# Mixture-of-experts attention block: a sine product on GpSimd waits for a sum on VectorE

## The chip, the core and the metric

The kernel runs on one core of one Trainium2 chip, as a single launch. The metric is the device time in microseconds (us). The core has engines that each run their own instruction queue in order and meet only through semaphores: TensorE (PE, matrix products), VectorE (DVE), ScalarE (ACT), GpSimd (POOL) and SyncE (SP, which starts transfers here). SBUF is the on-chip memory that they all read; PSUM is where TensorE leaves its products.

## The reference, cut to what matters

Input x is (4, 512, 256). It is normalised over its last axis, and the output is x plus an attention over 16 heads of size 128 plus a feed-forward part with eight routed experts (two chosen per row) and a shared one. The attention, with the rotation that the change touches:

```python
def _apply_rope(x, start_pos):
    ...
    x1 = x[..., 0::2]
    x2 = x[..., 1::2]
    r1 = x1 * cos - x2 * sin
    r2 = x1 * sin + x2 * cos
    return jnp.stack([r1, r2], axis=-1).reshape(B, T, H, Dh)
...
q = _apply_rope(q, 0)
k = _apply_rope(k, 0)
scores = jnp.einsum('bqhd,bkhd->bhqk', q, k) * scale
scores = jnp.where(causal[None, None, :, :], scores, jnp.float32(-jnp.inf))
attn = jax.nn.softmax(scores, axis=-1)
out = jnp.einsum('bhqk,bkhd->bqhd', attn, v).reshape(B, T, H * Dh)
return out @ wo
```

## The kernel before

All matrix products run in fp32, each as three products of a high and a low part (`hi*hi`, `hi*lo`, `lo*hi`). ScalarE writes the high part, and VectorE or GpSimd subtracts it to get the low one.

The attention is worked off as 64 heads m (a batch and a head each, `SLOTS`). The loop over steps s is software-pipelined and written out in each engine's own order: in step s, TensorE finishes head s, has the scores of heads s+1 and s+2 computed, and projects the key of head s+3 and the query of head s+4. One 128-row tile of the feed-forward part goes through most steps (s = -3 to 51). Routing (which experts each row takes) is computed by VectorE in steps 0 to 3; in steps 3 to 10 GpSimd sends the rows to a sorted table, four scatters a step; the rows come back by gathers on GpSimd, two a step from step 53, and sixteen in step 61.

The rotation of a query (which = 0) or a key (which = 1) of head m:

- TensorE projects into `qk_bank` (`project`).
- ScalarE copies it with its halves exchanged to `swapped[:, which]` (`swap`, L725).
- GpSimd multiplies `swapped[:, which]` by the sine table (`sin_product`, L876).
- VectorE multiplies `qk_bank` by the cosine table into `rot[:, which]` (`cos_product`, L1117).
- The two are added: for the query by VectorE (`rotate` in the vector block, L1124), for the key by GpSimd (`rotate` in the gpsimd block, L884).
- ScalarE writes the high part `qk_hi` (`rot_parts`, L734), GpSimd the low part `qk_lo` (`rot_parts`, L891).

`qk_bank` is one bank, so TensorE projects the key only after the query has been copied and multiplied, and the next query only after the key has.

GpSimd's queue in step s, in this order: sine product of the key of s+3, sum of the key of s+3, low part of the query of s+3, low part of its key, sine product of the query of s+4, and then weights, scatters or gathers of that step. VectorE's queue in step s holds, among much else: `row_max(s + 2, 3)` (L1133), the query's sum of s+3 (L1124), routing instructions in steps 0 to 3, the cosine product of the key of s+3 (L1117), two gating products, more maxima, the low parts of the transposed probabilities (L1148), two sums into the output rows (L1171), and last the cosine product of the query of s+4. ScalarE's queue in step s holds, around the rotation: `swap(s + 3, 1)`, an exponential, `rot_parts(s + 3, 0)`, copies, `rot_parts(s + 3, 1)`, `pt_parts(s + 1, 1)` (L756), `swap(s + 4, 0)`.

The routing instructions that the prediction names are L1030 (score, a scale and shift), L1035 (a maximum over the experts), L1036 and L1038 (comparison and product) in step 0, and L1072 (a copy) and L1074 (four sums) in step 2. L911 is a gather. L1228 adds gathered rows to the output.

Of the kernel before, what the change touches and what calls it, by code (L numbers as in the profile page):

```python
# [65 lines left out]
def moe_attention_kernel(nc, x_d, attn_d, ffn_d, wdown_d, gate_d, cos_d, sin_d, mask_d, ident_d,  # L66
                         iota_d, sel_d, out_d):
    with ExitStack() as ctx:
# [6 lines left out]
        def sem(name):  # L75
            return ctx.enter_context(nc.semaphore(name))
# [101 lines left out]
        cosm_ok, sinm_ok, rot_ok, rhi_ok, rlo_ok = ([sem(f"{n}_{x}") for x in "qk"] for n in (  # L178
            "cosm_ok", "sinm_ok", "rot_ok", "rhi_ok", "rlo_ok"))
# [37 lines left out]
        def exists(m):  # L217
            return 0 <= m < SLOTS
# [623 lines left out]
        def _(pool):  # L842
# [29 lines left out]
            def sin_product(m, which):  # L872
                if not exists(m):
                    return
                pool.wait_ge(swap_ok, 2 * m + which + 1)
                pool.tensor_tensor(swapped[:, which, :], swapped[:, which, :], sin_t[:, :],  # L876
                                   ALU.mult).then_inc(sinm_ok[which], 1)

# [36 lines left out]
            for s in range(-LEAD, SLOTS):  # L915
                q, r = prep(s)
                sin_product(s + 3, 1)
                rotate(s + 3, 1)
                rot_parts(s + 3, 0)
                rot_parts(s + 3, 1)  # L920
                sin_product(s + 4, 0)
                if s == -LEAD:
                    shared_parts()
                if r == 2:
                    weights_low(q)
                for n in scatter_steps(s):
                    scatter(n)
                for n in gather_steps(s):
                    gather(n)
                if s == -LEAD + 1:  # L930
                    pool.tensor_scalar(before[:, :], mask[:, T - P:T], -1.0, None, ALU.is_lt).then_inc(const_ok, 1)
# [434 lines left out]
```

## Time and profile before

| what | value |
|---|---|
| median of 3 runs | 805.72 us (805.53 to 807.64) |
| profiled execution, its own time | 804.73 us |
| its span | 802.9 us |
| mean granted clock of TensorE | 0.961 |
| busy: TensorE | 721.2 us (90%) |
| busy: VectorE | 664.4 us (83%) |
| busy: ScalarE | 593.2 us (74%) |
| busy: GpSimd | 504.2 us (63%) |
| sine products on GpSimd (L876) | 128, 175.7 us busy, mean 1372 ns |
| GpSimd idle just before them | 194.1 us |

The span is the time from the first to the last instruction of the profiled execution; its own time is 1.8 us more. A share of busy time is a mean over stages that differ: whether a delay counts is read from the chain of waits, which follows back from the last instruction what each had to wait for. A timeline row has the start in us from the span's start, the duration in us, the engine, the line, the operation with what it writes and reads, and in brackets how long the engine was idle before it and what ended that. An instruction may start some hundredths before the one ahead of it on its engine has ended.

### The profile page before, as it was taken

The numbers are of one execution on the slowest core, as the hardware profiler recorded it, in microseconds if no ns is written. First come the engines' busy times: TensorE is split into PE (matmuls) and PEld (weight loads), VectorE is DVE, ScalarE is ACT, GpSimd is POOL, SyncE is SP. The second block draws the span as 40 slices with busy tenths as digits, with TensorE's granted clock in tenths as the row PEclk, the third lists the DMA queues.
The fourth block names the chain that finished last, engine by engine and source line by source line (L and its number), as shares of the span: only waits on it lengthen the run. The fifth ranks groups of instructions, "written<-read, shape, count | busy, mean of one in ns | idle before, by whom it ended". The sixth has DMA issues, their size and how long they took to land.

```text
span 802.9 us, 15524 instructions
## 1 busy us (share of the span) xinstructions
PE 721.2 (90%) x4618; PEld 646.5 (81%) x4618; DVE 664.4 (83%) x1740; ACT 593.2 (74%) x1462; POOL 504.2 (63%) x413
## 2 busy tenths in 40 slices
PE   4798859898888999999999999999999999998633
PEld 3787758787777999999999999999999998886532
DVE  7667998888887888898888888988888888888526
ACT  3456647776876889888888888888888888886410
POOL 3444445888874666666656667666666667997730
PEclk9899998999999999999999999999999999999955
DMA  9342212344326445644445445644555430111212
GB/s 304 127 153 85 82 53 72 116 138 142 110 79 206 134 148 152 190 141 132 147 139 172 145 150 151 186 130 143 144 170 143 149 102 8 29 38 54 68 50 78
DMA packets 62066, 99.60 MB, mean 124 GB/s; under 512 B 9840, under 2 KB 34464, under 8 KB 61984
## 3 DMA queue, kind: packets, MB, share of 16 engines
q1 hardware_dynamic: 58912, 90.22, 36.8%
q0 software_dynamic: 3072, 8.39, 3.2%
q8 instruction: 38, 0.62, 0.3%
q14 instruction: 44, 0.36, 0.1%
HBM read 72.12 MB, written 26.48 MB: 123 GB/s over the span
## 4 chain that ended last, share of the span: by engine, by line
PE 66%; DVE 11%; POOL 10%; issue 5%; ACT 4%; another core or an unknown queue 2%; DMA 1%; DVEq 0%; SPq 0%; ACTq 0%; POOLq 0%
PE u_acc L403 13%; PE qk_proj L403 13%; PE scores L403 12%; PE ffn L403 10%; PE out_acc L403 8%; PE probs_t L509 7%; POOL swapped L876 3%; POOL qk_lo L891 2%; POOL rot L884 2%; DVE acc L1228 2%; DVE acc L1171 1%; POOL xs_sorted L900 1%; PE ffn L590 1%; PE ffn L564 1%
## 5 line engine op out<-in xcount | busy, mean ns | idle before, releaser
L876 POOL TENSOR_TENSOR swapped<-swapped,sin_t 128x512 f32<-128x512 f32 x128 | 175.7, 1372 | 194.1 <-ACT swapped L725 193.8
L891 POOL TENSOR_TENSOR qk_lo<-rot,qk_hi 128x512 fp32r<-128x512 f32 x128 | 165.4, 1299 | 26.6 <-ACT qk_hi L734 24.9
L1148 DVE TENSOR_TENSOR pt_lo<-probs_t,pt_hi 128x512 fp32r<-128x512 f32 (+3 forms) x256 | 125.4, 490 | 65.8 <-ACT pt_hi L756 64.1
L756 ACT ACTIVATE pt_hi<-probs_t 128x512 fp32r<-128x512 f32 (+3 forms) x256 | 111.8, 437 | 70.8 <-PE probs_t L509 39.0
L745 ACT ACTIVATE probs<-scores,nbias 128x512 f32<-128x512 f32 (+3 forms) x256 | 134.9, 527 | 36.6 <-DVE nbias L1133 35.1
L725 ACT ACTIVATE swapped<-qk_proj 64x512 f32<-64x512 f32 x256 | 151.9, 593 | 7.1 <-PE qk_proj L403 2.6
L1133 DVE CUSTOM_DVE_ANT_0 scores<-scores,mask 128x512 f32<-128x512 f32 (+3 forms) x256 | 125.3, 490 | 24.0 <-remote 13.2
L509 PE MATMUL probs_t<-ident,probs 128*128 128x128 f32 x640 | 114.5, 277 | 26.1 <-DVE pt_lo L1148 24.3
L1171 DVE SCALAR_TENSOR_TENSOR acc<-out_acc,rsum,acc 128x256 f32<-128x256 f32 x256 | 111.1, 476 | 8.4 <-remote 3.9
L509 PEld LDWEIGHTS probs_t<-ident,probs 128*128 128x128 f32 x640 | 81.0, 142 | 45.2 <-DVE pt_lo L1148 30.3
L884 POOL TENSOR_TENSOR rot<-rot,swapped 128x512 f32<-128x512 f32 x64 | 82.4, 1288 | 19.3 <-DVE rot L1117 11.0
L403 PE MATMUL scores<-qk_hi 128*128 128x512 f32 (+3 forms) x256 | 94.4, 369 | 0.0
L403 PE MATMUL u_acc<-pt_hi,c_hi 128*128 128x512 f32 (+3 forms) x256 | 89.4, 349 | 0.0
L1117 DVE TENSOR_TENSOR rot<-qk_proj,cos_t 128x512 f32<-128x512 f32 x128 | 87.3, 682 | 1.3 <-ACT swapped L725 1.2
L734 ACT ACTIVATE qk_hi<-rot 128x512 fp32r<-128x512 f32 x128 | 80.8, 631 | 4.8 <-POOL rot L884 4.2
L403 PE MATMUL u_acc<-pt_hi,c_lo 128*128 128x512 f32 (+3 forms) x256 | 84.2, 329 | 0.0
L403 PE MATMUL u_acc<-pt_lo,c_hi 128*128 128x512 f32 (+3 forms) x256 | 83.8, 328 | 0.0
L403 PE MATMUL scores<-qk_hi,qk_lo 128*128 128x512 f32 (+3 forms) x256 | 83.3, 325 | 0.0
L403 PE MATMUL scores<-qk_lo,qk_hi 128*128 128x512 f32 (+3 forms) x256 | 83.1, 325 | 0.0
L403 PE MATMUL out_acc<-m_hi,u_hi 128*128 128x256 f32 x256 | 79.0, 309 | 2.7 <-DVE u_lo L1156 2.4
L403 PE MATMUL out_acc<-m_hi,u_lo 128*128 128x256 f32 x256 | 73.5, 287 | 0.0
L403 PE MATMUL out_acc<-m_lo,u_hi 128*128 128x256 f32 x256 | 73.4, 287 | 0.0
(173 smaller groups left out, 1836.1 us busy)
## 6 DMA issues: line engine op xcount, KB each, us to landing
wt<-expert_parts SPq DMA_DIRECT2D x39, 704.0 KB, 4.5
wt<-expert_parts SPq DMA_DIRECT2D x39, 512.0 KB, 4.2
raw_a<-in_attn SPq DMA_DIRECT2D x8, 768.0 KB
xs_sorted<-u_lo SPq DMA_DIRECT2D x3, 1664.0 KB, 7.0
xs<-xs_sorted SPq DMA_DIRECT2D x39, 128.0 KB, 3.6
ys_sorted<-ysb SPq DMA_DIRECT2D x39, 128.0 KB, 4.0
expert_parts<-split SPq DMA_DIRECT2D x8, 352.0 KB, 2.3
expert_parts<-raw_f SPq DMA_DIRECT2D x8, 352.0 KB
```

Of the source, the lines that this page charges most:

```text
L403: last = pe.matmul(out, a, b, start=start and n == 0, stop=stop and n == 3 * len(pairs) - 1, **kw)
L509: last = pe.transpose(pt_bank[:, (i - j) * P:(i - j + 1) * P], probs[:, m % 2, a:a + P], ident[:, :])
L725: last = ac.activation(swapped[64 * half:64 * half + 64, which, :], qk_bank[64 - 64 * half:128 - 64 * half, :], ACT.Copy)
L745: ac.activation(probs[:, m % 2, PR_AT[i]:PR_AT[i] + n], s_bank[i % 2][:, 0:n], ACT.Exp, bias=nbias[:, m % 2, i:i + 1], scale=-1.0, accum_o ...
L756: ac.activation(pt_hi[:, PT_AT[j]:PT_AT[j] + n], pt_bank[:, 0:n], ACT.Copy).then_inc(pthi_ok, 1)
L876: pool.tensor_tensor(swapped[:, which, :], swapped[:, which, :], sin_t[:, :], ALU.mult).then_inc(sinm_ok[which], 1)
L884: pool.tensor_tensor(rot[:, which, :], rot[:, which, :], swapped[:, which, :], ALU.add).then_inc(rot_ok[which], 1)
L891: pool.tensor_tensor(qk_lo[:, m % 2, which, :], rot[:, which, :], f32(qk_hi[:, m % 2, which, :]), ALU.subtract).then_inc(rlo_ok[which], 1)
L1117: ve.tensor_tensor(rot[:, which, :], qk_bank[:, :], cos_t[:, :], ALU.mult).then_inc(cosm_ok[which], 1)
L1133: ve.tensor_tensor_reduce(a, a, mask[:, T - n:T], -SCALE, 3e38, ALU.add, ALU.min, nbias[:, m % 2, i:i + 1]).then_inc(max_ok, 1)
L1148: ve.tensor_tensor(pt_lo[:, c], pt_bank[:, 0:n], f32(pt_hi[:, c]), ALU.subtract).then_inc(ptlo_ok, 1)
L1171: ve.scalar_tensor_tensor(out=a, in0=out_bank[h][:, n, :], scalar=rsum[:, m % 4, i:i + 1], in1=a, op0=ALU.mult, op1=ALU.add).then_inc(add_ ...
```

## The change

The sine product of a key on GpSimd waits, besides for ScalarE's copy, until VectorE has added the two rotated parts of the query of the same head (`rot_ok[0]`, which L1124 raises). Both the sum and the product read SBUF only. No engine's sequence of instructions is altered; the second wait is an entry of its own in GpSimd's queue. The sine product of a query has no new wait. Behind the waiting instruction stand, on GpSimd, the key's sum, the two low parts and everything later.

```diff
--- before.py
+++ after.py
@@ -873,6 +873,9 @@
                 if not exists(m):
                     return
                 pool.wait_ge(swap_ok, 2 * m + which + 1)
+                if which == 1:
+
+                    pool.wait_ge(rot_ok[0], m + 1)
                 pool.tensor_tensor(swapped[:, which, :], swapped[:, which, :], sin_t[:, :],
                                    ALU.mult).then_inc(sinm_ok[which], 1)
```

## Rows read from the trace of the kernel before

**Rows 1.** The page: shares of the chain of waits by engine.
```profile
PE 66%; DVE 11%; POOL 10%; issue 5%; ACT 4%; another core or an unknown queue 2%; DMA 1%; DVEq 0%; SPq 0%; ACTq 0%; POOLq 0%
```

**Rows 2.** Timeline, head 31, steady stretch: start, us, engine, instruction.
```profile
410.71 0.69 DVE L1124 TENSOR_TENSOR rot<-rot,swapped 128x512 f32<-128x512 f32 x1
...
411.04 1.51 POOL L876 TENSOR_TENSOR swapped<-swapped,sin_t 128x512 f32<-128x512 f32 x1 [2.92 <-ACT swapped L725]
...
412.70 1.28 POOL L884 TENSOR_TENSOR rot<-rot,swapped 128x512 f32<-128x512 f32 x1
...
414.58 0.64 ACT L734 ACTIVATE qk_hi<-rot 128x512 fp32r<-128x512 f32 x1
```

**Rows 3.** Timeline, head 0.
```profile
29.50 0.68 DVE L1124 TENSOR_TENSOR rot<-rot,swapped 128x512 f32<-128x512 f32 x1
29.52 1.82 POOL L876 TENSOR_TENSOR swapped<-swapped,sin_t 128x512 f32<-128x512 f32 x1 [6.88 <-ACT swapped L725]
```

**Rows 4.** Chain of waits, heads 58 and 59: start, us, what.
```profile
694.07 1.33 POOL swapped L876
...
695.53 1.30 POOL rot L884
696.83 2.50 POOL qk_lo L891 x2
699.33 1.25 POOL swapped L876
...
700.73 0.99 POOL xn L911
...
704.44 1.30 POOL rot L884
```

**Rows 5.** Timeline, from head 58's ScalarE copy to head 59's product.
```profile
696.86 0.63 ACT L734 ACTIVATE qk_hi<-rot 128x512 fp32r<-128x512 f32 x1 [0.27 <-POOL rot L884]
...
699.16 0.68 DVE L1117 TENSOR_TENSOR rot<-qk_proj,cos_t 128x512 f32<-128x512 f32 x1
...
702.38 0.69 DVE L1124 TENSOR_TENSOR rot<-rot,swapped 128x512 f32<-128x512 f32 x1
...
703.00 1.30 POOL L876 TENSOR_TENSOR swapped<-swapped,sin_t 128x512 f32<-128x512 f32 x1
```

**Rows 6.** Timeline, heads 55 and 56.
```profile
668.85 1.30 POOL L884 TENSOR_TENSOR rot<-rot,swapped 128x512 f32<-128x512 f32 x1
...
670.18 0.63 ACT L734 ACTIVATE qk_hi<-rot 128x512 fp32r<-128x512 f32 x1 [0.22 <-POOL rot L884]
...
676.02 1.52 POOL L876 TENSOR_TENSOR swapped<-swapped,sin_t 128x512 f32<-128x512 f32 x1 [2.13 <-ACT swapped L725]
```

**Rows 7.** Chain of waits, heads 3 and 5.
```profile
74.67 1.24 DVE ysb L1030
...
76.58 0.30 DVE pick L1038
...
104.88 1.24 DVE xs L1072
```

**Rows 8.** Timeline, head 7.
```profile
136.61 0.69 DVE L1124 TENSOR_TENSOR rot<-rot,swapped 128x512 f32<-128x512 f32 x1
...
139.50 1.31 POOL L876 TENSOR_TENSOR swapped<-swapped,sin_t 128x512 f32<-128x512 f32 x1
```

**Rows 9.** Timeline from head 63 on; the last row is the chain's.
```profile
742.32 1.51 DVE L1124 TENSOR_TENSOR rot<-rot,swapped 128x512 f32<-128x512 f32 x1
743.75 0.68 DVE L1117 TENSOR_TENSOR rot<-qk_proj,cos_t 128x512 f32<-128x512 f32 x1
...
744.51 1.28 POOL L884 TENSOR_TENSOR rot<-rot,swapped 128x512 f32<-128x512 f32 x1 [1.23 <-DVE rot L1117]
...
769.78 0.95 POOL L911 DMA_INDIRECT wt<-ys_sorted,place  x1 [0.30 <-issue]
...
762.25 11.80 another core or an unknown queue
```

## The prediction

> **Names.** Head m is one of the 64 pairs of batch and head, in the order of `where`. Per head: D is VectorE's sum for the query (L1124), S GpSimd's sine product for the key (L876, the instruction that gets the new wait), C VectorE's cosine product for the key (L1117), G GpSimd's sum for the key (L884), A ScalarE's copy of the rotated key (L734), X GpSimd's two subtractions (L891).
>
> **What bounds the kernel now.** I read the chain of waits first, then timelines of VectorE, GpSimd and ScalarE around every S. TensorE holds 66% of the chain and GpSimd 10% [rows 1]. The reader is to see that GpSimd is not on it evenly. In heads 15 to 54 the chain is TensorE alone, with GpSimd idle before S. From head 56's S (676.02) to head 62's G it is GpSimd alone: S, G, two X, the next query's product, two gathers, and again [rows 4]. The change touches only S, so two questions decide: how much later does S end, and is that absorbed.
>
> **How much later S ends.** In the steady stretch S starts at 411.04, while D runs until 410.71 + 0.69 = 411.40 [rows 2]. With the wait it starts after D. The lag from VectorE's last event to a GpSimd start I take from head 63: C ends at 743.75 + 0.68 = 744.43 and G starts at 744.51, so 0.08 [rows 9]. The new start is 411.48, 0.44 later. But S is now stretched by the overlap: 1.51 us, against 1.30 where it meets only the last 0.07 of D [rows 2, 5]. At head 0 the two start 0.02 apart and S takes 1.82, ending 1.16 after D's end (30.18); in the steady stretch it ends 1.15 after [rows 2, 3]. So a product that overlaps is held until shortly before D ends. Afterwards it takes 1.30 at most, say 1.29, from 0.08 after D, ending 1.37 after: **0.22 us later**, not 0.44.
>
> By the Trainium skill's page "SBUF — State Buffer", section "Who interferes with whom", whichever of the two engines starts first keeps the shared ports for its whole instruction and the other is fully blocked. Taken literally, a held S would end 1.29 after D, and the wait would cost the lag of 0.08 alone; the sum below would be lower by 2 x 0.14 = 0.3. The rows show 1.15, and I go by them.
>
> **Heads 15 to 54, 40 heads: nothing.** S's delay moves G, which ends at 412.70 + 1.28 = 413.98, but A, which needs it, starts at 414.58 [rows 2]. ScalarE is late there by 0.60, more than 0.22. If the cover were gone, it would be 40 x 0.22 = 8.8 us: the slower end.
>
> **Heads 7 to 14: 0.1.** S starts at 139.50, long after D (136.61 + 0.69) [rows 8]; scatters stand ahead of it in GpSimd's queue. The wait is met, and leaves only one more entry in GpSimd's queue, between nothing and the lag of 0.08; I take 0.01 for each of 8 heads, near nothing since the engine has a scatter to work on meanwhile, and round up. Bounds 0 and 0.6.
>
> **Heads 0 to 6: -0.5.** Two things turn round here. Where S began first, D waited for it (as at head 63, 1.51 instead of 0.69 [rows 9]); heads 4 and 6 look so too, but TensorE has no gap there, so I count nothing. Where D began first, the routing instruction behind D waited for S: at head 3 the one of L1030 takes 1.24 on the chain, at head 5 the one of L1072 also 1.24, where a routing instruction of that size takes 0.30 (L1038) [rows 7]. With S behind D they come through first: 0.95 each, and VectorE holds the chain. But two and four more routing instructions with two inputs in SBUF follow. They now meet S themselves and end just after it, so most of it is given back: at head 3 S would end 1.37 after D, at 76.04, where the third instruction of the row now ends at 76.88; two of 0.30 that can only end behind 76.04, the first of them nearly done by then, end at 76.5 (D ends where L1030 begins on the chain, at 74.67). That is 0.4; at head 5, with S again at its end, 0.1. Together -0.5, bounds 0 and -1.9.
>
> The same page and section says that a VectorE instruction with two SBUF inputs contends with a GpSimd instruction that reads SBUF, and a reduction does not. That speaks for giving back; without it the term would be -1.9 and the sum -0.5.
>
> **Heads 55 and 56: +0.4.** Here G's delay is no longer covered: G of head 55 ends at 668.85 + 1.30 = 670.15 and A starts at 670.18 [rows 6]. A's delay goes to ScalarE's next copies, VectorE's C for the next query and TensorE's projection. Head 56's S (676.02, 1.52 long) is the chain itself [rows 6]. Two times 0.22, less a little slack: 0.4, bounds 0.2 and 0.44.
>
> **Heads 57 to 62: +0.9.** GpSimd comes to S only when its gathers are out, at 703.00, and D ends at 702.38 + 0.69 = 703.07 [rows 5]. Looked at alone the wait costs 0.15 once. But D itself follows from the G before: G ends at 696.83, A starts at 696.86, C at 699.16 and D at 702.38 [rows 4, 5], with every engine passing it on at once. So the delay comes round. The new loop is G to D's end, 703.07 - 695.53 = 7.54, plus 0.08, plus S 1.30, plus 0.14 from S to G (694.07 + 1.32 to 695.53) = 9.06. The old loop is 704.44 - 695.53 = 8.91 [rows 4, 5]. That is **0.15 a head, six times**. If a step of the way from G to D had slack, it would be 0.15 once: the lower bound.
>
> **Head 63 and the tail: 0.** D waited for S and took 1.51; now 0.69, so VectorE and ScalarE gain 0.82. GpSimd does not: D would end at 743.01, S at 743.09 + 1.29 = 744.38, G starts 0.14 later at 744.52, against 744.51 [rows 9]. The 18 gathers behind it, to the one at 769.78, keep their place. VectorE stands from 762.25 for 11.80 us for a queue that the profile does not name [rows 9], until 774.05, when the last gather must just have landed. So the end follows GpSimd, and the 0.82 is lost in that stall. What is lost before goes through whole.
>
> **Sum.** 0.1 - 0.5 + 0.4 + 0.9 = +0.9 us. The profiled execution is 804.73 us (span 802.9 and 1.8 around it), so 805.6; the median of the runs is 805.72, so I forecast **806.6 us**.
>
> **Rivals.**
> First, the other side of my forecast: VectorE's release pays in full. The routing instructions behind do not meet S (-1.9 instead of -0.5), and the tail follows VectorE, so head 63 gives -0.8. Then 0.1 - 1.9 + 0.4 + 0.9 - 0.8 = -1.3: 804.4, faster. It decides if L1036 and L1074 run beside S at 0.3. For it speaks that VectorE holds the chain at heads 3 and 5 [rows 7]; against it the stretched pairs in [rows 2, 3].
> Second, slower: the 0.22 is not covered in the steady stretch, +8.8 and so some 815. It decides if A is ready before G. Against it stand 0.60 us in every such head.
> Third, and faster too, the stall in the tail is not bound to the gathers' end. VectorE reaches it 0.8 us earlier than GpSimd does its gathers, and might get a piece of work done before it. From 774.05 to the span's end at 802.9 there are 29 us of work; 4 of them done within the stall would give 802.6.
> Fourth, the change does next to nothing: the loop has slack, each part is met, 805.8. Against it the shared start of S and D in 40 heads [rows 2].
>
> **Numbers.** My forecast 0.62 (its own range 805.6 to 807.6), the first rival 0.18, the second 0.07, the third 0.06, the fourth 0.07. The range 804.2 to 808.2 takes in my forecast, the first rival and the fourth, and leaves out the other two, 0.13, and some of the edges. About 0.3%, 2.4 us, is what a measurement of this kernel can tell from no change. Within it lie the forecast, the first and the fourth, less their edges: 0.83. Slower by more: the second and an edge, 0.10. Faster by more: the third and an edge, 0.07.
>
> **What would show it.** S starts 0.08 after D in heads 15 to 62 and takes 1.29 to 1.31; S and D never overlap, and D is never longer than 0.7. G to G in the steady heads is what it was, and some 9.06 in heads 57 to 62. At head 3 the L1030 instruction takes 0.3 and the one behind the next is long. G of head 62 lies some 0.9 later than it did. I am wrong if the loop of heads 57 to 62 stays at 8.91, if the steady heads grow, or if the stall of the tail starts or ends elsewhere against the gathers.

## The result, and the profile after

| | before | after |
|---|---|---|
| median | 805.87 us (20 runs, 805.16 to 808.89) | 809.61 us (20 runs, 804.48 to 814.73) |
| ratio | | 1.0040 (95%: 1.0024 to 1.0057) |
| profiled execution, its own time | 804.73 us | 814.73 us |

The kernel became slower by 0.4%, some 3.2 us, where 0.9 was forecast; that is above the 0.3% from which a loss can be told, which had a chance of 0.10. The change as a whole was timed twice more, on two chips: 1.0041 (1.0023 to 1.0059, run all1) and 1.0023 (1.0003 to 1.0043, all2). The three together give 1.0036, uncertain by 0.0010: **2.9 us, give or take 0.8**. That is the number to explain, not the 10 us between the two profiled executions: the one of after is the slowest of its 20 runs. Of its 10 us, 7.2 lie before G of head 17 (270.16 against 262.93), in a stretch that varies between executions of one and the same kernel (last section), 1.5 lie between heads 54 and 62, 0.1 in the step to head 63 and 1.2 behind it.

The page of after: the chain's shares, and the group of the sine products.

```profile
PE 66%; DVE 13%; POOL 7%; issue 6%; ACT 4%; another core or an unknown queue 2%; DMA 1%; DVEq 0%; SPq 0%; ACTq 0%; POOLq 0%
...
L879 POOL TENSOR_TENSOR swapped<-swapped,sin_t 128x512 f32<-128x512 f32 x128 | 165.4, 1292 | 222.4 <-DVE rot L1127 177.1
```

Against [rows 1] GpSimd has gone from 10% of the chain to 7%, and VectorE and the issue share have grown by as much: GpSimd is waited for less, because it now waits itself. The sine product's mean fell from 1372 to 1292 ns, so it is hardly ever stretched any more (3 of the 128 take over 1.32 us), and what GpSimd waits for before it is now VectorE's sum. (Lines behind the edit have moved by 3 in after and by 2 or 3 in the experiments.)

Timeline of after, head 31, in the steady stretch.

```profile
417.66 0.69 DVE L1127 TENSOR_TENSOR rot<-rot,swapped 128x512 f32<-128x512 f32 x1
...
418.49 1.29 POOL L879 TENSOR_TENSOR swapped<-swapped,sin_t 128x512 f32<-128x512 f32 x1 [3.43 <-DVE rot L1127]
...
419.92 1.30 POOL L887 TENSOR_TENSOR rot<-rot,swapped 128x512 f32<-128x512 f32 x1
...
421.52 0.64 ACT L734 ACTIVATE qk_hi<-rot 128x512 fp32r<-128x512 f32 x1
```

D ends at 418.35 and S starts at 418.49: 0.14 later, not the 0.08 of the forecast. S ends 1.43 after D's end, where the held S of [rows 2] ended 1.15 after it: **0.28 later, not 0.22**. G ends at 421.22, and A starts 0.30 after that, where it was 0.60. The cover holds, and is half used up. From G of head 17 to G of head 54 it takes 394.68 us before (262.93 to 657.61) and 394.68 after (270.16 to 664.84): nothing of the delay is passed on there.

Timeline of after, from D of head 59 to A.

```profile
710.28 0.69 DVE L1127 TENSOR_TENSOR rot<-rot,swapped 128x512 f32<-128x512 f32 x1
...
711.11 1.30 POOL L879 TENSOR_TENSOR swapped<-swapped,sin_t 128x512 f32<-128x512 f32 x1 [0.25 <-DVE rot L1127]
...
712.55 1.29 POOL L887 TENSOR_TENSOR rot<-rot,swapped 128x512 f32<-128x512 f32 x1
713.88 0.63 ACT L734 ACTIVATE qk_hi<-rot 128x512 fp32r<-128x512 f32 x1 [0.49 <-POOL rot L887]
```

The chain of waits of after, one turn of the loop, from G of head 58 to G of head 59.

```profile
703.42 1.31 POOL rot L887
...
704.75 0.05 ACT qk_hi L734
...
705.29 0.48 ACT pt_hi L756
...
705.80 0.57 DVE pt_lo L1151
...
707.14 0.74 PE u_acc L403 x3
...
707.88 0.93 PE qk_proj L403 x3
...
708.93 0.71 PE scores L403 x3
...
710.28 0.14 DVE nbias L1136
710.42 0.55 DVE rot L1127
710.98 0.02 issue
711.00 0.02 POOLq L878
711.02 0.10 issue
711.11 1.31 POOL swapped L879
...
712.44 0.02 POOLq L886
```

In [rows 4] this turn was GpSimd alone. Now the chain leaves GpSimd at G and comes back to it at S: through ScalarE (A, and the copy of the probabilities behind A), VectorE, TensorE, the maximum of scores, and D. This is the loop that the prediction priced, though its middle runs through ScalarE's probability copy (L756) and the scores, not through C. A turn is 712.55 - 703.42 = 9.13 (G in the timeline above and in the chain): G to D's end 7.55, then 0.14, S 1.30, and 0.14 to G. The forecast had 7.54, 0.08, 1.30 and 0.14. The one term that differs is the lag. The chain shows what it is made of: an entry of 0.02 in GpSimd's own queue (L878, the new wait) with 0.02 before it and about 0.10 behind. S to G has the same shape (L886) and the same 0.14, before and after: there the wait for S is an entry of its own too.

Timeline of after, head 63, and the last gather.

```profile
751.07 0.69 DVE L1127 TENSOR_TENSOR rot<-rot,swapped 128x512 f32<-128x512 f32 x1
751.68 0.68 DVE L1120 TENSOR_TENSOR rot<-qk_proj,cos_t 128x512 f32<-128x512 f32 x1
751.91 1.28 POOL L879 TENSOR_TENSOR swapped<-swapped,sin_t 128x512 f32<-128x512 f32 x1 [4.28 <-DVE rot L1127]
753.34 1.28 POOL L887 TENSOR_TENSOR rot<-rot,swapped 128x512 f32<-128x512 f32 x1
...
778.83 0.95 POOL L914 DMA_INDIRECT wt<-ys_sorted,place  x1 [0.30 <-issue]
```

The longest piece of the chain of waits of after in the tail.

```profile
772.65 10.39 another core or an unknown queue
```

D is 0.69 where it was 1.51 [rows 9], and G follows S, as forecast. The stall ends at 783.04, 3.3 us after the last gather is out (779.78); before, 774.05 against 770.73, 3.3 too. VectorE's 0.82 shows no gain at the end. The distance of 3.3 us is not the same in every run (last section).

### The profile page after: what moved, and what is told of

Read it like the earlier page. It is cut to its first block, busy times and chain, and to the rows that moved or that the text cites. A ratio compares the mean times of both kernels' runs of the same rounds, so it can differ in the third digit from the quotient of the medians.

```text
span 812.9 us, 15588 instructions
## 1 busy us (share of the span) xinstructions
PE 729.2 (90%) x4618; PEld 653.3 (80%) x4618; DVE 663.3 (82%) x1740; ACT 593.5 (73%) x1462; POOL 492.9 (61%) x413
## 4 chain that ended last, share of the span: by engine, by line
PE 66%; DVE 13%; POOL 7%; issue 6%; ACT 4%; another core or an unknown queue 2%; DMA 1%; DVEq 0%; SPq 0%; ACTq 0%; POOLq 0%
PE u_acc L403 13%; PE qk_proj L403 13%; PE scores L403 12%; PE ffn L403 10%; PE out_acc L403 8%; PE probs_t L509 7%; POOL swapped L879 3%; POOL rot L887 2%; POOL xs_sorted L903 2%; DVE acc L1174 2%; DVE acc L1231 2%; PE ffn L590 1%; DVE pt_lo L1151 1%; PE ffn L564 1%
## 5 line engine op out<-in xcount | busy, mean ns | idle before, releaser
L879 POOL TENSOR_TENSOR swapped<-swapped,sin_t 128x512 f32<-128x512 f32 x128 | 165.4, 1292 | 222.4 <-DVE rot L1127 177.1
L756 ACT ACTIVATE pt_hi<-probs_t 128x512 fp32r<-128x512 f32 (+3 forms) x256 | 111.8, 437 | 74.6 <-PE probs_t L509 43.8
```

Source lines behind the costliest of these rows:

```text
L756: ac.activation(pt_hi[:, PT_AT[j]:PT_AT[j] + n], pt_bank[:, 0:n], ACT.Copy).then_inc(pthi_ok, 1)
```

## The experiments

One table from the traces carries the argument. It gives, in us, the time from G of head 54 to G of head 62, the mean turn from head 56 to 62, the step from G of 62 to G of 63, and beside them the timed ratio. All three are differences of starts of G in the timeline.

| run | 54 to 62 | per head | 62 to 63 | ratio (95%) |
|---|---|---|---|---|
| before | 73.53 | 8.91 | 13.37 | |
| same_kernel | 73.53 | 8.91 | 12.47 | 0.9996 (0.9980 to 1.0012) |
| after | 75.07 | 9.12 | 13.43 | 1.0040 (1.0024 to 1.0057) |
| all1 | 75.00 | 9.11 | 13.41 | 1.0041 (1.0023 to 1.0059) |
| all2 | 75.06 | 9.12 | 13.43 | 1.0023 (1.0003 to 1.0043) |
| early | 73.46 | 8.90 | 13.22 | 0.9992 (0.9978 to 1.0006) |
| mid | 73.22 | 8.90 | 12.47 | 1.0004 (0.9985 to 1.0023) |
| late | 75.33 | 9.12 | 13.42 | 1.0039 (1.0022 to 1.0056) |
| late62 | 75.32 | 9.12 | 13.35 | 1.0040 (1.0025 to 1.0054) |
| late57 | 74.77 | 9.12 | 13.20 | 1.0021 (1.0004 to 1.0038) |
| late63 | 73.49 | 8.90 | 12.73 | 0.9993 (0.9977 to 1.0009) |
| waits_swapped | 74.67 | 9.06 | 13.38 | 1.0007 (0.9992 to 1.0022) |
| waits_swapped2 | 74.59 | 9.05 | 13.37 | 1.0009 (0.9987 to 1.0031) |
| padding | 74.40 | 9.06 | 13.33 | 1.0015 (1.0000 to 1.0029) |
| padding2 | 75.21 | 9.19 | 13.34 | 1.0017 (0.9997 to 1.0037) |
| sum_first | 74.40 | 9.13 | 12.27 | 1.0026 (1.0012 to 1.0040) |
| sum_early | 72.81 | 8.90 | 12.26 | 0.9997 (0.9982 to 1.0013) |
| early_sum_no_wait | 73.20 | 8.92 | 12.13 | 0.9994 (0.9980 to 1.0008) |
| late_gathers | 73.06 | 8.83 | 8.83 | 1.0103 (1.0078 to 1.0128) |
| late_gathers_wait | 74.99 | 9.11 | 9.11 | 1.0160 (1.0140 to 1.0180) |

### Where the loss is: the wait for some heads only

The whole change again, then the wait for a part of the heads:

```diff
+                if which == 1:                      # all1
+                if which == 1 and m <= 6:           # early
+                if which == 1 and 7 <= m <= 54:     # mid
+                if which == 1 and m >= 55:          # late
+                    pool.wait_ge(rot_ok[0], m + 1)
```

> The whole change once more. Loop theory: heads 57 to 62 run at 9.12 us each in every execution instead of 8.91, heads 55 and 56 lose 0.3 each, nothing else moves by itself, so the kernel is 1.5 to 2 us slower than before in executions with the same granted clock (some 807.5), and what is more than that comes with a lower mean clock. Clock theory: the wait itself brings more stretches at half clock in the stage up to 260 us; then the median is again some 4 us above before, and the trace again has half-clock stretches near 65 and 235 us.

> The wait for heads 0 to 6 alone. Loop theory: 805.5 to 806, no change (at head 3 the two-input instruction behind takes the place of the stretched one, 0.3 gained; heads 4 and 5 lose 0.2). Clock theory: most of the loss is here, because heads 0 to 6 shift TensorE's idle stretches: 808 to 809.

> The wait for heads 7 to 54 alone. Loop theory: no change, 805.9, as the key's sum is ready before ScalarE asks for it in heads 15 to 54 and the wait is met in heads 7 to 14. Clock theory: 806 to 808, if the half-clock stretch near 235 us comes from the entries in GpSimd's queue at heads 7 to 14.

> The wait for heads 55 to 63 alone. Loop theory: all of the steady loss is here, 807.4 to 807.9, with 9.12 us from sum to sum in heads 57 to 62. Clock theory: below 807.5, a third of the loss or less.

Measured on one chip: before 804.54, all1 807.87, early 804.30, mid 805.35, late 808.20. The loss is in heads 55 to 63 whole. The 48 heads of mid cost nothing that can be measured, so the second rival falls: a 0.28 that is covered by 0.60 costs nothing, 40 times over. (The traces say it more sharply: from G of head 17 to G of head 54 all twenty runs take 394.65 to 394.69 us, with the wait or without.) Early is not measurably faster: its interval (0.9978 to 1.0006) holds the 0.9994 of the forecast's -0.5, and just leaves out the 0.9976 of the first rival's -1.9. The clock theory named in these expectations falls with them: it put most of the loss into the early heads, where there is none, and a third or less into the late ones, where all of it is.

### Which of the last heads

```diff
+                if which == 1 and 55 <= m <= 62:    # late62
+                if which == 1 and m == 63:          # late63
+                if which == 1 and 57 <= m <= 62:    # late57
```

> The wait for heads 55 to 62 alone, not 63. Loop theory: the whole loss, from sum to sum 9.12 us in heads 57 to 62, some 1.8 us lost between the sum of head 54 and that of head 62, and the median 1.8 to 3 us above before. Tail theory (a good part of the loss comes from head 63, where VectorE comes earlier to the stall): half of that or less.

> The wait for head 63 alone. Loop theory: no loss; the sum of head 63 starts at the same time behind that of head 62 (13.4 us), and the stall in the tail still ends some 3.3 us after the last gather is out: ratio 1.000. Tail theory: 1.2 to 1.5 us slower, ratio 1.0015 to 1.002.

> The wait for heads 57 to 62 alone: the loop of 9.12 without the two single delays of heads 55 and 56. Loop theory: 1.25 us by head 62, ratio 1.0016. If the rest hangs on heads 57 to 62, some 1.003.

late62 carries the loss, and head 63 nothing. By head 62, late62 is 75.32 - 73.53 = 1.79 us behind before, and late57 74.77 - 73.53 = 1.24, which is six turns of 0.21. The 0.55 between them is heads 55 and 56, twice the 0.28 of an S that was held and now waits. (In after this reads as 0.27, because G of head 54 is itself already 0.28 late there, under A's cover; late62 has no wait before head 55, so it shows the whole.) Their timed ratios, on two chips, are too wide apart to add to this.

### The order of the two waits

```diff
+                if which == 1:
+                    pool.wait_ge(rot_ok[0], m + 1)
                 pool.wait_ge(swap_ok, 2 * m + which + 1)
                 pool.tensor_tensor(swapped[:, which, :], ...
```

> The whole change, but the new wait is written ahead of the one for ScalarE's copy, so that it is the instruction's own wait and not the entry ahead of it. Lag theory: the product then starts 0.08 us behind VectorE's sum instead of 0.14, and the loop of heads 57 to 62 is 9.06 us, as I had forecast, instead of 9.12: 0.4 us less loss. If the lag is VectorE's alone, it stays at 0.14 and 9.12.

> waits_swapped once more. Its first ratio of 1.0007 was lower than its trace says: 1.1 us more than the kernel before by head 62. Lag theory: 9.06 us a head again, and 1.001 to 1.002, between no wait and the change as it is (1.0036 over three comparisons).

Timeline of waits_swapped, D and S of one head and G of that head.

```profile
706.68 0.69 DVE L1126 TENSOR_TENSOR rot<-rot,swapped 128x512 f32<-128x512 f32 x1
...
707.45 1.30 POOL L878 TENSOR_TENSOR swapped<-swapped,sin_t 128x512 f32<-128x512 f32 x1 [0.19 <-DVE rot L1126]
708.89 1.30 POOL L886 TENSOR_TENSOR rot<-rot,swapped 128x512 f32<-128x512 f32 x1
```

D ends at 707.37 and S starts at 707.45: 0.08. I read it so: of two waits the one coded second is an entry of its own ahead of the instruction, and the one coded first goes with the instruction itself. Where VectorE's sum is the last to come and its wait is the entry, the instruction has still to be started behind it; where it goes with the instruction, it releases it at once. The turn is 9.06, the forecast's number to the hundredth. Both runs together give 1.0008, uncertain by 0.0012. That is less than the whole change's 1.0036, and by more than the traces say: these put only 0.4 us between the two orders by head 62, and the ratios 2.3, give or take 1.3. The rest of that gap I leave open.

### Is it the wait, or just a longer turn?

No wait here; GpSimd writes a constant again into a tile of ones ahead of S (in padding2 into a second one too, `chosen`, which is no longer read in these steps).

```diff
+                if 55 <= s + 3 <= 62:
+                    pool.memset(ones[:, :], 1.0)
```

> The kernel before, without the new wait, but GpSimd clears a small tile (128x128 bf16, 0.20 us at the start of the kernel) ahead of the key's sine product of heads 55 to 62. Loop theory: the loop of heads 57 to 62 grows from 8.91 to some 9.11 us with nothing else changed, 1.2 us by head 62, and the kernel loses what a longer loop costs: 1.2 us, or some 2.5 if a longer loop brings a lower mean clock with it, as in the runs with the wait. Rival (the wait costs something besides the loop): at most 1.2 us, ratio 1.0015 or below.

> As padding, but GpSimd clears two small tiles ahead of the key's sine product of heads 55 to 62; no wait. The loop of heads 57 to 62 is some 9.25 us, 2 us by head 62. If each us of the loop costs one us at the end, ratio 1.0025 to 1.003; if the rest comes with a longer loop whatever makes it long, 1.004 or more; if it comes with the wait alone, 1.0025.

GpSimd's timeline in padding.

```profile
702.11 0.23 POOL L918 MEMSET ones<- 128x128 bf16 x1
702.28 1.31 POOL L876 TENSOR_TENSOR swapped<-swapped,sin_t 128x512 f32<-128x512 f32 x1
703.73 1.29 POOL L884 TENSOR_TENSOR rot<-rot,swapped 128x512 f32<-128x512 f32 x1
```

0.23 of work lengthens the turn by 0.15 and the way to head 62 by 0.87 us; the time grows by 1.2 us (of 786), with an interval of 0.0 to 2.3. padding2 is 1.68 behind by head 62, nearly late62's 1.79, and costs 1.4 us (-0.2 to 3.0), less than was expected; all2, on the same chip, 1.8. In the traces nothing special to the wait is needed to lengthen the turn. That a us put into these turns comes out as a us at the end fits both timings, but they are too coarse to show it.

### Does the loop need a full GpSimd?

The rival was that the wait costs only because GpSimd is full in these heads. Here all 32 gathers stand in step 61, and the first rows are added in step 62, so that GpSimd has slack; the second kernel has the change as well.

```diff
-            n, last = 2 * (s - GATHER_AT), 2 * (61 - GATHER_AT)
-            return range(n, n + 2) if 0 <= n < last else range(last, TOP_K * TT) if s == 61 else ()
+            return range(0, TOP_K * TT) if s == 61 else ()
...
-                if s in (59, 62, 63, 64):
-                    add_routed({59: 0, 62: 1, 63: 2, 64: 3}[s])
+                if s in (62, 63, 64):
+                    for b0 in {62: (0, 1), 63: (2,), 64: (3,)}[s]:
+                        add_routed(b0)
```

> The kernel before, but with all 32 gathers in step 61 and the first two adds of gathered rows in step 62. GpSimd is no longer the bound in heads 57 to 62: from sum to sum some 8.83 us, as from head 55 to 56 before. The tail grows by the 16 gathers, 20 us.

> The same with the wait. Loop theory: the loop through VectorE's sum is the bound in both, and the wait makes it 9.11 instead of 8.83: 0.28 a head for heads 55 to 62, 2.2 us against the run without the wait. Rival (only GpSimd's full queue makes the wait cost): no difference, as GpSimd has nothing to catch up with.

Timeline of late_gathers, without the wait.

```profile
704.29 1.30 POOL L883 TENSOR_TENSOR rot<-rot,swapped 128x512 f32<-128x512 f32 x1
...
711.13 0.69 DVE L1123 TENSOR_TENSOR rot<-rot,swapped 128x512 f32<-128x512 f32 x1
...
711.46 1.51 POOL L875 TENSOR_TENSOR swapped<-swapped,sin_t 128x512 f32<-128x512 f32 x1 [2.13 <-ACT swapped L724]
713.11 1.30 POOL L883 TENSOR_TENSOR rot<-rot,swapped 128x512 f32<-128x512 f32 x1
```

Timeline of late_gathers_wait, the same piece of a head.

```profile
717.02 0.69 DVE L1126 TENSOR_TENSOR rot<-rot,swapped 128x512 f32<-128x512 f32 x1
...
717.85 1.29 POOL L878 TENSOR_TENSOR swapped<-swapped,sin_t 128x512 f32<-128x512 f32 x1 [2.66 <-DVE rot L1126]
719.28 1.29 POOL L886 TENSOR_TENSOR rot<-rot,swapped 128x512 f32<-128x512 f32 x1
```

GpSimd idles 2.13 us before S, and still the wait lengthens the turn, from 8.83 to 9.11: by the whole 0.28. So the rival falls. S is on the loop through D whether GpSimd is full or not, and there the loop has no slack: 7.53 from G to D's end (711.82), 1.15 to the end of a held S, 0.14 to G, which is 8.82 of 8.83. A full GpSimd had in fact taken off some of the cost: there S started late anyway, and only 0.21 was left of the 0.28. (As a whole both kernels lose, since 32 gathers one behind the other then stand between head 63 and the end; that is the price of the move, not of the wait.) Between the two, 2.2 us were expected, and the traces show 2.2 by G of head 63 (1.93 by head 62, 0.28 in the step after it). The timed ratios lie further apart, 0.0057 or 4.5 us, give or take 2.5; what more than 2.2 of it is, these runs do not tell.

### Taking D out of the loop

The wait stays, and D moves forward in VectorE's queue for heads from 55: in sum_first ahead of the maximum of scores, in sum_early further, right behind the sums that begin the step; early_sum_no_wait has sum_early's order without the wait.

```diff
+                if s + 3 >= 55:
+                    rotate(s + 3, 0)
...
-                rotate(s + 3, 0)
+                if s + 3 < 55:
+                    rotate(s + 3, 0)
```

> The whole change, and VectorE adds the query's parts ahead of the row maximum in place of behind it, for heads 55 to 63. Loop theory: VectorE's sum ends some 0.6 us earlier, is done when GpSimd comes with its gathers out, and the loop falls back to GpSimd's own 8.91 to 8.93 us; the loss goes, ratio 1.000 to 1.001. If the loss came from the clock or from the tail, it stays at 1.004.

> The whole change, and VectorE adds the query's parts of heads 55 to 63 right behind its sums into the output rows, still earlier than in sum_first. Port theory (in sum_first the second gather took 1.12 us instead of 0.95 because VectorE's sum ran over its start): the sum now ends before that gather starts, the gather takes 0.95 again, the loop is GpSimd's own 8.91 us, and the loss goes: ratio 0.999 to 1.001. Rival: the loop is at 9.08 again, 1.002 or more.

> The kernel before without the wait, with VectorE's sum of the query of heads 55 to 63 placed right behind its sums into the output rows, as in sum_early. The sum then ends before the sine product starts, so that the product of heads 55 and 56 takes 1.29 us instead of 1.52, and head 63's sum is no longer held. Port theory: the way from the sum of head 54 to that of head 62 is 72.8 us as in sum_early, 0.7 less than before, and head 63 gives 0.5 to 1 more: ratio 0.998 to 0.999, faster than both kernels. Rival: GpSimd's own queue bounds all of it, ratio 1.000.

Timeline of sum_first: D, and GpSimd's second gather, S and G around it.

```profile
702.42 0.68 DVE L1127 TENSOR_TENSOR rot<-rot,swapped 128x512 f32<-128x512 f32 x1
...
702.80 1.12 POOL L914 DMA_INDIRECT raw_f<-ys_sorted,place  x1 [0.30 <-issue]
703.93 1.29 POOL L879 TENSOR_TENSOR swapped<-swapped,sin_t 128x512 f32<-128x512 f32 x1
705.37 1.30 POOL L887 TENSOR_TENSOR rot<-rot,swapped 128x512 f32<-128x512 f32 x1
```

Timeline of sum_early, the same pieces.

```profile
704.48 0.69 DVE L1127 TENSOR_TENSOR rot<-rot,swapped 128x512 f32<-128x512 f32 x1
...
705.40 0.95 POOL L914 DMA_INDIRECT raw_f<-ys_sorted,place  x1 [0.30 <-DVE rot L1127]
706.36 1.30 POOL L879 TENSOR_TENSOR swapped<-swapped,sin_t 128x512 f32<-128x512 f32 x1
707.81 1.30 POOL L887 TENSOR_TENSOR rot<-rot,swapped 128x512 f32<-128x512 f32 x1
```

In sum_first D is done (703.10) long before S could start, and S waits for nothing: the loop is open. But the turn has not fallen back to 8.91: it is 9.41 once, from head 56 to 57, and 9.07 from there on (9.13 is the mean of the six). D now runs over the start of the second gather, which takes 1.12 to 1.14 instead of 0.95. GpSimd is full, so that is 0.17 on its own turn. This run was expected at 1.000 to 1.001 and came out at 1.0026, though by G of head 63 it is not behind before (74.40 + 12.27 against 73.53 + 13.37); what its 2.1 us are made of is open. In sum_early D ends at 705.17, before the gather begins at 705.40, and the turn is back at 8.90: the wait costs nothing (0.9997). Without the wait the same order is at 0.9994, where 0.998 to 0.999 was expected, and takes 73.20 from head 54 to 62 instead of the expected 72.8. Its interval (0.9980 to 1.0008) allows a small gain and shows none, so no version measurably beats the kernel before.

### The same kernel twice

No edit at all.

> The kernel before itself, unchanged, as one of the kernels compared with it. It gives the scatter of such a comparison: ratio within 0.999 to 1.001 of one if the 0.4% seen four times with the wait in heads 55 to 62 is more than scatter. Its trace shows how far two executions of one kernel lie apart before head 54.

> The whole change once more, beside the kernel before as its own rival. Loop theory alone: 1.8 us by head 62, ratio 1.0023, and no more. With the rest (something else costs 1 to 2 us): 1.004 again.

0.9996: the comparison finds no difference where there is none. Its step from head 62 to 63 is 12.47, where before has 13.37, and here the two traces show why.

Windows of before, from 8.5 to 10.5 us after G of head 62, and the same of same_kernel (columns: window, its length, busy time and instructions of PE, PEld, DVE, ACT and POOL, then PEclk, which is TensorE's granted clock, DMA share, GB/s).

```profile
739.64:741.64 2.00, 1.80 (x5) 1.51 (x6) 1.23 (x4) 1.55 (x5) 0.00 (x0) 0.55 0.84 274
...
744.29:746.29 2.00, 1.80 (x8) 1.62 (x9) 1.83 (x5) 1.70 (x5) 0.00 (x0) 0.93 0.82 278
```

In this window TensorE computes the scores whose maximum stands ahead of D in VectorE's queue. With the granted clock at 0.55 of full speed (it falls to half, 1.2 GHz, within the window) the three score products take 1.62 us and D of head 63 starts 11.18 after G of head 62; at 0.93 they take 0.94 and D starts at 10.50. The other runs fall into the same two groups. Of the 15 traces with before's order of instructions, three have a clock of 0.86 to 0.93 in this window and a step of 12.47 to 12.73 (same_kernel, mid, late63), and twelve have 0.50 to 0.61 and a step of 13.20 to 13.43. All ten with a longer turn are among the twelve, and so are before and early. The long step so goes with an earlier fall of the clock, which two of five executions without a longer turn have as well. On average it is 0.5 longer with the longer turn (13.37 against 12.85), in padding too, so it is no effect of the wait itself. Whether these 0.5 reach the end is not shown: from G of head 62 to the end of the span the five without a longer turn take 70.3 us (69.7 to 71.8), and the nine with one, padding left out since its chip has a shorter tail, 70.6 (68.5 to 73.0).

## Why the prediction was wrong

The mechanism was right in its place and kind: the cover of heads 15 to 54, the two single delays of heads 55 and 56, and a loop of six turns. What failed is the **sum**, in the two terms that carry it. The lag of 0.08 behind the loss terms is 0.14, and the gain of 0.5 in heads 0 to 6 is not there. With both mended, and heads 7 to 14 at 0, the sum is +1.8 instead of +0.9. The rest of the measured 2.9 is in no term of the prediction, and its cause is open.

- *The lag of 0.08*: wrong for this wait. I took it from head 63's C to G, where no entry stands between. The new wait is coded second and is an entry of its own, as the section on the change says: 0.14. waits_swapped alone brings 0.08 back. So S ends 0.28 later, not 0.22. The prediction's own rows held the right number: it took S to G as 0.14 from [rows 4] in the same sum.
- *Heads 57 to 62, "0.15 a head, six times"*: the loop and the full six repetitions are confirmed by late57 and late_gathers_wait, its way round through A by the chain of after; the size is 0.21, so 1.25 instead of 0.9.
- *Heads 55 and 56, +0.4*: 0.55 (late62 against late57), 2 x 0.28.
- *Heads 0 to 6, -0.5*: not there (early, 0.9992 with 0.0014 on either side, would allow it; the traces speak against it). The chain of after, heads 3 and 5:

```profile
77.42 0.15 DVE ysb L1033
77.59 0.30 DVE best L1038
77.91 1.09 DVE pick L1039
79.03 0.30 DVE pick L1041
...
107.02 1.43 DVE xs L1077
```

  As argued, L1033 no longer meets S (0.15 for 1.24) and a later one does (1.09 for 0.30): at head 3, from D's end to the end of the instruction that the prediction calls the third (it is the fourth behind D, L1041 in after), 79.33 - 77.42 = 1.91 against 76.88 - 74.67 = 2.21 [rows 7], a gain of 0.3 for the 0.4 forecast. At head 5 the 1.43 takes the place of 1.24 [rows 7], and by the timelines VectorE's C starts 2.60 after D instead of 2.56: nothing. And at head 4, which I had not counted, a routing instruction (L1046, 1.36 on the chain) now meets S, and 0.2 is lost. Together near zero. The first rival, with -1.9, falls by these rows and, narrowly, by early.
- *Heads 7 to 14, 0.1, and 15 to 54, 0*: right (mid, 1.0004, 0.0019 on either side, and the 394.68 us from head 17 to 54 in both traces). A's margin went from 0.60 to 0.30.
- *Head 63 and the tail, 0*: right for head 63 within what is timed (late63, 0.9993, 0.0016 on either side). Not foreseen is that the step from head 62 to 63 takes one of two lengths, by when TensorE's clock falls, and that all runs with a longer turn have the long one; the profiled execution of before had it too, so the prediction's rows could not show it.

By the traces the sum is 0.55 + 1.25 = 1.8 us by head 62, against the 1.3 of the forecast's two terms there: 0.06 x 8 = 0.5 more, for the lag. Another 0.4 is heads 0 to 14 (-0.5 and 0.1, now 0), which leads from 0.9 to 1.8. The three timings give 2.9, give or take 0.8, and late and late62, with 1.0039 and 1.0040, say much the same. The 1.1 between is what the account lacks. The step to head 63 can be up to 0.5 of it. Over the whole way from G of head 54 to the end of the span, the five traces without a longer turn average 143.8 us (143.2 to 145.3) and the five with the wait in all of heads 55 to 62 146.1 (143.7 to 148.1): 2.3, but each group spreads over more than the piece that is missing.

With the lag and heads 0 to 6 right, the forecast would have been some 807.5, inside the stated range up to 808.2, and still 2 us under the median of 809.61. So these two terms alone do not explain that the range was missed. The lag should have had a bound of 0.14 from my own rows (I had one row of 0.08, and took it for a constant), and the sum a term for what a delay does behind head 62.

The fourth rival (the loop has slack) falls by late57 and late_gathers_wait. The third (VectorE gets 4 us of work done within the stall) falls by late63, which gives it the unhindered D of head 63 and gains nothing that can be measured; its premise, that the stall's end is not tied to the last gather, is not refuted (last section).

On the rule of the Trainium skill's page "SBUF — State Buffer", section "Who interferes with whom", that whichever engine starts first blocks the other fully (the page words the full block for VectorE's two-port modes, and says of an instruction with two SBUF inputs, as D is, that it contends): a held S ended 1.15 after D, where being blocked to the end would make it 1.29 or more, in every steady head of before (1.13 to 1.15). The measurement decides, and going by it was right for the price: by the rule the cost per held S is 0.14, by the rows 0.28, and late62 against late57 showed 0.55 for two in the traces.

## What to carry to other kernels

A wait for an engine that itself waits, some steps on, for what the waiting instruction brings forth closes a loop; its price is not the idle time once but the lengthening of the turn, times the turns that have no slack. So work out the turn: the way from the result back to the awaited instruction, the lag, the instruction itself. Take the lag from a wait that stands in the same position in the queue as the new one. If such a wait must be there, put it first and the awaited work earlier, and look at what that work then runs beside. And where a delay ends in a stretch whose length differs between executions by more than the delay, price it to the edge of that stretch, and say that what is behind is not priced.

## What the runs showed of the hardware

- From the end of VectorE's instruction to GpSimd's start: 0.14 us where the awaited semaphore is coded last of two, 0.08 where it is coded first.
- A sum on VectorE that reads two tiles of SBUF lengthens a gather that GpSimd starts during it, from 0.95 to between 1.12 and 1.14 us (sum_first, heads 57 to 62), and not one that starts behind it (sum_early).
- The stall in the tail, put down to an unknown queue, is no fixed piece. In the 16 traces of the other chips VectorE's longest idle piece there is 6.9 to 11.8 us, mostly with a second one behind a short piece of work, and the last ends 1.4 us (all2, waits_swapped) to 3.8 us after the last gather is out. On one chip it is absent: neither padding nor sum_early has an idle piece of VectorE over 2.5 us there, and before has a median of 786.12 on it, against 804.5 to 808.1 on the others. What the queue is, no run told.
- TensorE's granted clock at the start differs between executions of one kernel. From 20 to 60 us it was 0.87 in before and 0.79 in same_kernel, and from 60 to 100 us 0.96 and 0.91. G of head 17 came 4.67 us later in same_kernel, though the program is the same and the medians agree; from there to head 54 both take the same time.

Windows of before and of same_kernel (columns as above).

```profile
20.00:60.00 40.00, 34.75 (x212) 31.13 (x212) 27.53 (x53) 21.59 (x45) 17.65 (x14) 0.87 0.44 141
...
20.00:60.00 40.00, 37.49 (x217) 34.32 (x217) 26.50 (x52) 20.38 (x41) 16.74 (x13) 0.79 0.43 141
```

Such differences make a single profiled execution a poor measure of a change of 0.3%; the change is better read as differences within one stretch of a trace.
